# A delta-rule attention kernel: k·k and k·q as one product of 256 columns, and half of the output product one step later

## The reference, cut to what matters

```python
q, k, v = silu(conv(...))               # causal convolution over 4 tokens
q = l2norm(q) * DK ** -0.5; k = l2norm(k)
state = state * exp(g)
delta = (v - k @ state) * beta
state = state + outer(k, delta)
out   = q @ state                       # per token, one after the other
core  = rmsnorm(out) * norm_weight * silu(z);  x = x + core @ W_out
```

## Time and profile before

| | us |
|---|---|
| median of 3 runs | 2876.93 |
| lowest, highest | 2876.19, 2879.32 |
| the profiled execution: its own time | 2879.55 |
| the profiled execution: span from first to last instruction | 2877.8 |
| granted TensorE clock, mean over the span | 0.966 |

### The profile page before, as it was taken

The page is one execution under the profiler, slowest core; times in us unless marked ns, Lnnn a source line. Parts: engine busy times, 40 slices in busy tenths (PEclk is TensorE's granted clock), DMA queues, the critical chain, the costliest instruction groups (busy, mean ns, idle before and its releaser), DMA issues. The chain is left out here.

```text
span 2877.8 us, 62476 instructions
## 1 busy us (share of the span) xinstructions
PE 2646.5 (92%) x21920; PEld 2193.3 (76%) x21921; DVE 1883.1 (65%) x3550; ACT 1358.7 (47%) x4371; POOL 693.0 (24%) x967
## 2 busy tenths in 40 slices
PE   5999995748999999999999999999999997699997
PEld 4999994435777777777777777777777776699997
DVE  4111114889999999999999999999987543311111
ACT  1111111525666666666666666666665553011111
POOL 1222221531223122221322222232221111122221
PEclk9999996969999999999999999999999997699999
DMA  6767662545554645555554554645553323576674
GB/s 226 240 220 229 213 197 55 177 159 154 181 172 146 194 145 170 168 165 163 164 174 151 178 163 153 187 141 182 157 152 111 102 70 112 196 229 213 224 223 135
DMA packets 412290, 488.67 MB, mean 170 GB/s; under 512 B 215488, under 2 KB 295872, under 8 KB 412032
## 3 DMA queue, kind: packets, MB, share of 16 engines
q1 hardware_dynamic: 397056, 464.86, 49.8%
q0 software_dynamic: 14976, 20.46, 4.6%
HBM read 348.64 MB, written 138.67 MB: 169 GB/s over the span
## 5 line engine op out<-in xcount | busy, mean ns | idle before, releaser
L530 PE MATMUL f_ps_up<-f_xgT,f_w_up 128*128 128x128 f32 x4368 | 504.9, 276 | 2.5 <-DMA f_w_up<-in_L_ffn_w_dram 2.5
L530 PEld LDWEIGHTS f_ps_up<-f_xgT,f_w_up 128*128 128x128 f32 x4368 | 498.2, 193 | 3.4 <-ACT f_xgT L568 3.3
L597 DVE TENSOR_TENSOR f_hT<-f_hT,f_ps_up 128x512 f32<-128x512 f32 (+1 forms) x156 | 96.9, 621 | 499.7 <-ACT f_hT L576 499.7
L1544 DVE SCALAR_TENSOR_TENSOR at_qk<-at_bank,at_taps_qk,at_qk 128x510 f32<-128x510 f32 (+2 forms) x384 | 282.0, 744 | 35.0 <-ACT at_qk L1418 25.9
L1544 DVE SCALAR_TENSOR_TENSOR at_vT<-at_bank,at_taps_v,at_vT 128x510 f32<-128x510 f32 (+2 forms) x384 | 280.5, 744 | 35.8 <-ACT at_vT L1425 26.7
L576 ACT ACTIVATE f_hT<-f_ps_up 128x512 f32<-128x512 f32 (+1 forms) x156 | 84.9, 544 | 433.5 <-PE f_ps_up L530 433.5
L1814 POOL TENSOR_SCALAR at_small<-at_small 128x4 f32<-128x4 f32 x64 | 15.3, 238 | 1101.8 <-ACT at_squares L1452 1101.7
L1220 PE MATMUL at_bank<-xnT,at_w_qk 128*128 128x512 f32 x512 | 253.7, 619 | 11.0 <-DVE at_qk L1544 7.6
L494 POOL DMA_INDIRECT sums<-f_y,f_row_of x78 | 123.7, 1586 | 541.3 <-DVE f_y L603 541.3
L541 PE MATMUL f_ps_y<-f_w_down,f_hT 128*128 x1092 | 250.5, 381 | 3.8 <-DVE f_hT L597 3.8
L1245 PE MATMUL at_bank<-at_w_vz,xnT 128*128 128x256 f32 x1024 | 243.6, 381 | 8.3 <-DVE at_vT L1544 8.2
(11 more groups left out here) (221 smaller groups left out, 5428.0 us busy)
## 6 DMA issues: line engine op xcount, KB each, us to landing
f_w_up<-in_L_ffn_w_dram SPq DMA_DIRECT2D x156, 896.0 KB, 6.4
at_steps_e<-steps_kept SPq DMA_DIRECT2D x64, 512.0 KB, 6.7
mt_kept<-at_mt_made SPq DMA_DIRECT2D x64, 512.0 KB, 4.2
pt_kept<-at_pt_made SPq DMA_DIRECT2D x64, 512.0 KB, 3.1
at_mt<-mt_kept SPq DMA_DIRECT2D x64, 512.0 KB, 4.0
at_pt<-pt_kept SPq DMA_DIRECT2D x64, 512.0 KB, 4.5
qk_kept<-at_qk SPq DMA_DIRECT2D x64, 256.0 KB, 2.9
ks_kept<-at_ks_made SPq DMA_DIRECT2D x64, 256.0 KB, 2.7
```

Source lines behind the costliest of these rows:

```text
L530: last = te.matmul(ps_up[hf][w][:, at:at + P], w_up[b][:, w, k, P * j:P * j + P], xgT[b][:, k, :], start=(k == 0), stop=(k == KD - 1))
L597: v.tensor_tensor(part, part, ps_up[hf][1][:, 0:P * (high - low)], ALU.mult).then_inc(h_ready, 1)
L1544: ins = v_.scalar_tensor_tensor(out=dst[:, :, back:], in0=src[:, :, 0:SEQ - back], scalar=taps[:, 3 - back:4 - back], in1=dst[:, :, back:] ...
```

## The change

Three things are changed. First, `products` makes kᵀk and kᵀq of one tile of tokens by a single matmul with 256 moving columns (k and q side by side), instead of two with 128. For this the banks of gen[0] and gen[2] are now the two halves of one tensor `pair`, half 0 of `products` (tiles 0 and 1) goes to one and half 1 (tiles 2 and 3) to the other. Both `mix` now wait for both halves and read `pair` with a stride, and both banks are free only when both `mix` are through. Second, `output 1` becomes `late_output`: PE issues it in the next step, after `inv_x 32`; its reader `join` moves on DVE from the end of a step to the next step, behind `inv_x 32`. Third, in DVE_ORDER the piece `blocks 2` moves from behind `add 1` to ahead of `add 0`.

```diff
-    "join": -1, "lift": -1,
-    "norm": -2, "norm_scale": -2, "shape": -2,
+    "lift": -1,
+    "late_output": -2, "join": -2, "norm": -2, "norm_scale": -2, "shape": -2,
...
-PE_ORDER = (("inv_x", 32), ("solve", 0), ("proj_qk", 0), ("state",), ("inv_n",), ("proj_qk", 1), ("y_turn", 0),
+PE_ORDER = (("inv_x", 32), ("late_output",), ("solve", 0), ("proj_qk", 0), ("state",), ("inv_n",), ("proj_qk", 1), ("y_turn", 0),
...
-DRAIN_PE_ORDER = (("solve", 0), ("inv_last",), ("inv_x", 32), ("state",), ("on_state", 0), ("on_state", 1),
+DRAIN_PE_ORDER = (("late_output",), ("solve", 0), ("inv_last",), ("inv_x", 32), ("state",), ("on_state", 0), ("on_state", 1),
...
-        bank = [r.ps(f"bank{k}", [P, 512]) for k in range(8)]
-        proj_bank, inv_bank, gen = bank[0:2], bank[2:4], bank[4:8]
+        bank = [r.ps(f"bank{k}", [P, 512]) for k in range(6)]
+        pair = r.ps("pair", [P, 2 * 512])
+        proj_bank, inv_bank = bank[0:2], bank[2:4]
+        gen = [pair[:, 512:1024], bank[4], pair[:, 0:512], bank[5]]
...
                 def bank0_read(u, me):
...
+                    at_least(pe, s["mt_ready"], seen(u, me, ("products", 1)))
                     at_least(pe, s["pt_ready"], seen(u, me, ("products", 1)))
...
                     at_least(pe, s["mt_ready"], seen(u, me, ("products", 0)))
+                    at_least(pe, s["pt_ready"], seen(u, me, ("products", 0)))
...
-                    (bank0_read if of else bank2_read)(u, me)
-                    q, k = qk[two(u)][:, 0, :], qk[two(u)][:, 1, :]
-                    for t in range(Q4):
+                    (bank0_read if half else bank2_read)(u, me)
+                    for t in (2 * half, 2 * half + 1):
                         tt = slice(P * t, P * t + P)
-                        last = te.matmul(gen[0 if of else 2][:, tt], k[:, tt], q[:, tt] if of else k[:, tt], start=True, stop=True)
-                    last.then_inc(s["kq_done" if of else "kk_done"], 1)
+                        last = te.matmul(pair[:, 256 * t:256 * t + 256], qk[two(u)][:, 1, tt], qk[two(u)][:, :, tt], start=True, stop=True)
+                    last.then_inc(s["kk_kq_done"], 1)
...
-                    dve.wait_ge(s["kq_done" if of else "kk_done"], idx(u) + 1)
+                    dve.wait_ge(s["kk_kq_done"], 2 * idx(u) + 2)
...
-                    both = gen[0 if of else 2][:].rearrange("p (t m) -> p t m", m=P).unsqueeze(2).to_broadcast([P, Q4, HV, P])
+                    kq_kk = pair[:].rearrange("p (t a m) -> p t a m", a=2, m=P)
+                    both = kq_kk[:, :, 0 if of else 1, :].unsqueeze(2).to_broadcast([P, Q4, HV, P])
```

More of the change, by code:

```diff
@@ L868 @@
             ("spill",), ("load_qk",), ("load_vz",))
-PE_ORDER = (("inv_x", 32), ("solve", 0), ("proj_qk", 0), ("state",), ("inv_n",), ("proj_qk", 1), ("y_turn", 0),
+PE_ORDER = (("inv_x", 32), ("late_output",), ("solve", 0), ("proj_qk", 0), ("state",), ("inv_n",), ("proj_qk", 1), ("y_turn", 0),
             ("on_state", 0), ("on_state", 1), ("inv_x", 64), ("turn", 1), ("y_turn", 1), ("project", 0), ("turn", 0),
             ("project", 1), ("proj_v", 2), ("proj_v", 3), ("solve", 1), ("inv_last",), ("products", 0),
-            ("products", 1), ("z", 0), ("turns", 0), ("z", 1), ("turns", 1), ("output", 0), ("output", 1))
+            ("products", 1), ("z", 0), ("turns", 0), ("z", 1), ("turns", 1), ("output", 0))
 ACT_ORDER = (("weigh", 0), ("norm",), ("copy_state",), ("conv_qk", 0), ("inv_n",), ("y_copy", 0), ("conv_qk", 1),
@@ L876 @@
              ("turn_copies", 1), ("z_gate", 0), ("lift",), ("z_gate", 1), ("gate_qk", 1))
-DVE_ORDER = (("inv_x", 32), ("blocks", 0), ("blocks", 1), ("conv_qk", 0), ("conv_qk", 1), ("inv_x", 64), ("add", 0),
-             ("from_state",), ("add", 1), ("blocks", 2), ("blocks", 3), ("conv_v", 2), ("conv_v", 3), ("scan",),
-             ("mix", 0), ("mix", 1), ("shape",), ("join",))
+DVE_ORDER = (("inv_x", 32), ("join",), ("blocks", 0), ("blocks", 1), ("conv_qk", 0), ("conv_qk", 1), ("inv_x", 64), ("blocks", 2),
+             ("add", 0), ("from_state",), ("add", 1), ("blocks", 3), ("conv_v", 2), ("conv_v", 3), ("scan",),
+             ("mix", 0), ("mix", 1), ("shape",))
 POOL_ORDER = (("scales",), ("diag",), ("scales_rest",), ("out_weights",), ("norm_scale",), ("low",))
@@ L886 @@
                   ("inv_n",), ("z", 0), ("inv_x", 64), ("products", 1), ("turns", 0), ("turns", 1), ("z", 1),
-                  ("output", 0), ("output", 1))
+                  ("output", 0))
 DRAIN_ACT_ORDER = (("weigh", 0), ("copy_state",), ("from_state",), ("y_copy", 0), ("y_copy", 1), ("norm",),
@@ L891 @@
                    ("gate_qk", 1), ("z_gate", 0), ("z_gate", 1), ("inv_last",), ("turn_copies", 1), ("lift",))
-DRAIN_DVE_ORDER = (("from_state",), ("inv_x", 32), ("blocks", 0), ("add", 0), ("conv_qk", 0), ("blocks", 1),
+DRAIN_DVE_ORDER = (("join",), ("from_state",), ("inv_x", 32), ("blocks", 0), ("add", 0), ("conv_qk", 0), ("blocks", 1),
                    ("add", 1), ("conv_v", 2), ("conv_v", 3), ("scan",), ("inv_x", 64), ("mix", 0), ("mix", 1),
-                   ("blocks", 2), ("conv_qk", 1), ("join",), ("shape",), ("blocks", 3))
+                   ("blocks", 2), ("conv_qk", 1), ("shape",), ("blocks", 3))
 DRAIN_POOL_ORDER = (("scales",), ("diag",), ("scales_rest",), ("norm_scale",), ("out_weights",), ("low",))
@@ L1201, in bank2_read @@
                     at_least(pe, s["mt_ready"], seen(u, me, ("products", 0)))
+                    at_least(pe, s["pt_ready"], seen(u, me, ("products", 0)))
                     at_least(pe, s["rhs_ready"], seen(u, me, ("on_state", 0)))
-                    at_least(pe, s["joined"], seen(u, me, ("output", 1)))
+                    at_least(pe, s["joined"], seen(u, me, ("late_output",)))
                 def bank3_read(u, me):
@@ L1257, in turn, with products @@
                     last.then_inc(s["qk_turned"], 1)
-                def products(u, of):
-                    me = ("products", of)
+                def products(u, half):
+                    me = ("products", half)
                     pe.wait_ge(s["qk_ready"], 2 * idx(u) + 2)
-                    (bank0_read if of else bank2_read)(u, me)
-                    q, k = qk[two(u)][:, 0, :], qk[two(u)][:, 1, :]
-                    for t in range(Q4):
+                    (bank0_read if half else bank2_read)(u, me)
+                    for t in (2 * half, 2 * half + 1):
                         tt = slice(P * t, P * t + P)
-                        last = te.matmul(gen[0 if of else 2][:, tt], k[:, tt], q[:, tt] if of else k[:, tt], start=True, stop=True)
-                    last.then_inc(s["kq_done" if of else "kk_done"], 1)
+                        last = te.matmul(pair[:, 256 * t:256 * t + 256], qk[two(u)][:, 1, tt], qk[two(u)][:, :, tt], start=True, stop=True)
+                    last.then_inc(s["kk_kq_done"], 1)
                 def turns(u, half):
@@ L1369, in output @@
                     pe.wait_ge(s["w_ready"], 2 * idx(u) + 1 + ch)
-                    (bank2_read if ch else bank1_read)(u, ("output", ch))
+                    (bank2_read if ch else bank1_read)(u, ("late_output",) if ch else ("output", 0))
                     for b in range(2):
@@ L1376, in output, with late_output @@
                     last.then_inc(s["o_psum"], 1)
+                def late_output(u):
+                    output(u, 1)
                 def y_turn(u, half):
@@ L1404, in _ @@
                           "inv_x": inv_x, "inv_n": inv_n, "inv_last": inv_last,
-                          "solve": solve, "state": state_, "on_state": on_state, "output": output, "y_turn": y_turn,
+                          "solve": solve, "state": state_, "on_state": on_state, "output": output, "late_output": late_output, "y_turn": y_turn,
                           "project": project})
@@ L1414, in conv_qk @@
                     act.wait_ge(s["qk_projected"], 2 * idx(u) + ct + 1)
-                    at_least(act, s["kq_done"], idx(u) - 1)
+                    at_least(act, s["kk_kq_done"], 2 * (idx(u) - 1))
                     at_least(act, s["qk_stored"][two(u)], 16 * (of_two(u) - 1))
```

2 lines of the change are left out of this document (1 added, 1 removed).

## The result

The changed kernel takes 2889.12 us (median of 6 runs, 2886.76 to 2892.72); the kernel before, run beside it, 2880.39 us. The ratio is 1.0035, with a 95% interval of 1.0025 to 1.0046: slower by about 10 us (the two medians are 8.7 apart). Three of the kernels further down had one run each, of 3966, 7195 and 3168 us, in a slower state of the chip; the medians and ratios there leave it out. The forecast was 2875 with a range of 2862 to 2887. The time lies outside the range and on the other side of the old kernel. In the profiled execution the span is 2889.0 us against 2877.8.

The account below looks back on a forecast made before the run. PE bounds the kernel, DVE having 8% left; with the third part, a loop through `add 0`. Steps A to D of 27.72, 28.02, 27.77, 27.77 make a round 111.28, not 111.43; times 11.75, -1.8 us off 2876.93: 2875, range 2862 to 2887.

Parts of the forecast that it names:

- The first part, 1.97 instead of 2.00: PE's `products`: wide matmuls take 1.97 us, not 2.00, as half 1 still waits for `weigh 1`; saves 0.03 a step.
- The strided `mix`: DVE's two `mix` reading both banks with a stride: 0 extra taken, upper bound 0.3 us more for each.
- The second part, nothing: Late output on PE and `join` on DVE: work only moves, so the cost is nothing.
- wait for P: At `late_output` on PE: P from `mix` 1, ended 1552.39, is there before the request at 1552.90 - 0.03; no loss.
- The third part, a loop through `add 0`: From one `proj_v` over DVE's `blocks 2` and `add 0` to the next: 28.02 us in kind B, 27.77 in C and D.
- Rival 1: PE never waits for `add 0`; every step 27.45 us, round 109.80, 19 us saved, 2858; chance 0.20.
- `blocks 2` is two copies of 0.38, 0.60 in a row: DVE's `blocks 2` in kind B, inside the loop through `add 0`: 0.60 us, giving a loop of 28.02.
- Kind A's term: DVE's `blocks 2` in kind A, 2.64 us (1512.90 to 1515.54): `proj_v` 0.20 late, step 27.72.
- C and D: Steps of these two kinds: loop through `add 0` of 27.77 us each, with `blocks 2` at 2.20.
- the way back: From `add 0`'s end on DVE to `proj_v` on PE: 0.12 us taken, rows giving 0.05 and 0.25.
- Rival 3: Dearer loop through `add 0`: strided `mix` 0.15 more each gives 2886, way back 0.13 more gives 2881; chance 0.21.
- The forecast's own range: Around 2875: way back -3 to +6 us, wait in `products` -2.4 in kind A; 2870 to 2882, chance 0.54.

Follow-up runs that it names:

- the last two kernels: Changed kernel with `blocks 2` early in A, late in B, halved in C and D: 2862.57 us; same with `z 0` between the `products` halves: 2861.86 us.

## Why the forecast was wrong

Timeline of PE, changed kernel, a step of kind C: `products`, `z 0`, `late_output`, `solve 0`.

```profile
1577.33 2.09 PE L1270 MATMUL at_pair<-at_qk 128*128 128x256 f32 x8
1579.26 1.89 PE L1249 MATMUL at_bank<-at_w_vz,xnT 128*128 128x256 f32 x8
...
1585.19 1.16 PE L1377 MATMUL at_pair<-at_wv,at_pt 128*128 128x128 f32 x8
1586.19 1.06 PE L1345 MATMUL at_pair<-at_vr,at_invT 128*128 128x128 f32 x8
```

1. *The first part, 1.97 instead of 2.00.* Nearly right: 1.93 (1577.33 to 1579.26 in the kind C step). The second half starts 0.99 after the first and not 1.04, which is 0.21 after `weigh 1` ends where it was 0.25, though the change adds a wait ahead of it. The strided `mix` costs nothing, as taken. What the forecast did not see is that both `mix` now hold both banks, so that this part by itself would cost 32 us.
2. *The second part, nothing.* Right by itself (0.9998), and `late_output` does not wait for P: it starts 0.12 us after the last row of `inv_x 32`, as `solve 0` did in the kernel before, and its four matmuls take 1.00. That "the same four matmuls, `join` and nothing else move" was too little said, since the move takes the wait out of point 1.
3. *The third part, a loop through `add 0`.* The mechanism is there in B, C and D, as the waits on `add 0` show, and undoing this part alone brings back the old time. `conv_v` has idle time ahead of it in all four kinds, as forecast. Rival 1, no loop, is ruled out.
4. *The step that failed: "`blocks 2` is two copies of 0.38, 0.60 in a row".* It was 1.61 (1542.57 to 1544.18). The duration was taken from a place in which nothing held the copies up, and carried to one beside GpSimd's `affine_select`. Of the 1.01 us too little, 0.90 is the hold (1.28 for the second copy instead of 0.38) and 0.11 the way of counting in point 6. Twelve rounds of 0.90 are 11 us, about all of the loss. Experiments showed it: away from that place 0.38, in another form in the same place 0.60 and unheld.
5. *Kind A's term, 2.64 for `blocks 2`,* took the time of both its pieces, 1512.90 to 1515.54, where only one moves: 1.30. `proj_v` does not wait in A, the step is 27.40 and not 27.72.
6. *C and D* are 0.14 and 0.15 above the forecast: `blocks 2` costs 2.31 from start to start where I took 2.20. That was from the reduction's start to that of `conv_v`, which starts 0.08 before the reduction's end (1571.11, 1571.19), while `add 0` starts 0.02 after it (1572.07, 1572.09). And the way back was 0.15 and not 0.12.

By kinds that is -0.32 + 1.05 + 0.14 + 0.15 = +1.02 a round, and 111.28 + 1.02 is what was measured, 112.30. Rival 3, a dearer loop, named the sign and, with 2886, nearly the time, but by luck: both of its prices (a strided `mix`, a long way back) were wrong. `mix` is as it was, and the way back is 0.03 longer than taken. The forecast's own range, up to 2882, adds up to 2881; that changes nothing.

A row of the kernel before should have warned me, and I had not read it. Beside the two copies of kind B, in their old place (1541.67 to 1542.34), the POOL timeline of before has

```profile
1541.81 0.63 POOL L1830 TENSOR_SCALAR at_small<-at_small 128x4 f32<-128x4 f32 x1
```

and in the changed kernel, where the copies are gone from there, the same instruction reads

```profile
1545.27 0.23 POOL L1837 TENSOR_SCALAR at_small<-at_small 128x4 f32<-128x4 f32 x1
```

The copies already held up GpSimd, by 0.40 us; the round did not pay for it there.

About 1.7 us of the 11.2 in the span come after the last `state`. They can't be put down to the change: over the twelve profiles this stretch takes 492.8 to 495.0 us, and the last two kernels, alike there, are 1.9 apart (494.7 and 492.8). The same holds for the 1.1 us ahead of the sixth `state`, which lies between 827.95 and 834.74. What stays open is why kind B stays at 27.74 where its copies are out of the loop.

## What to carry to other kernels

The duration of an instruction belongs to its place. Before a piece is moved, look at what the other engines do at the place it goes to, GpSimd above all, and ask for each instruction of the piece whether it can run beside them at its own length. And a piece that is different in each kind of step (here 1.30 us in A, about 0.7 in B, 2.3 in C and D) wants a place by kind: ahead of the gate only what is shorter than the slack of the loop, the rest in the idle time behind it. That turned +10 us into -18.

## What was not expected of the hardware

- A VectorE copy and a tensor_tensor of 256 values per partition took 1.28 and 1.51 us beside a GpSimd `affine_select` that had started first, 0.38 and 0.66 alone; they ended 0.24 and 0.45 us after it. A reduction of as many values took 0.60 in the same place, as alone, and was over before it.
- The trace shows the held instruction as longer, not as idle time ahead of it.
- The other way round the same copies stretched a small GpSimd tensor_scalar from 0.23 to 0.63 us, and the `affine_select` from 1.10 to 1.26.
- Reading PSUM across two banks in pieces of 128 with a stride of 256 went at the pace of reading one bank straight: 1.22 us for 1024 values.
